# Two softmax attentions of a decoder: where TensorE waits for the copied values, and which queue loads one batch's packed keys

## The reference

```python
q = jnp.einsum('bsd,hkd->bhsk', x, wq.reshape(H, dk, D))
k = jnp.einsum('bsd,hkd->bhsk', x, wk.reshape(H, dk, D))
v = jnp.einsum('bsd,hkd->bhsk', x, wv.reshape(H, dk, D))
q = _apply_rope(q, sin, cos)
k = _apply_rope(k, sin, cos)
scores = jnp.einsum('bhqk,bhsk->bhqs', q, k) / jnp.sqrt(jnp.asarray(dk, x.dtype))
scores = jnp.where(causal, -jnp.inf, scores)
...
x = x + _L1_attn_ref(_layernorm(x, axis=-1), L1_attn_wq, L1_attn_wk, L1_attn_wv, L1_attn_wo)
```

```python
logits = jnp.einsum('bqhd,bkhd->bhqk', q, k) * scale
w = jax.nn.softmax(logits, axis=-1)
attn = jnp.einsum('bhqk,bkhd->bqhd', w, v)
```

## Time and profile before

| | |
|---|---|
| time of one execution, median of 3 runs | 1608.46 us (1607.88 to 1609.58) |
| time of the profiled execution | 1609.24 us |
| its span, first to last instruction | 1607.4 us |
| PE busy | 1131.6 us (70%) |
| DVE busy | 1060.7 us (66%) |
| ACT busy | 496.2 us (31%) |
| POOL busy | 575.2 us (36%) |
| mean granted TensorE clock | 0.870 of full speed |

### The profile page before, as it was taken

One profiled execution on the slowest core, in us unless ns is written; L12 is line 12 of the kernel. 1 busy time (PEld: TensorE's weight loads), 2 busy tenths in 40 slices (PEclk: granted clock), 3 DMA queues, 4 the chain that ended last, 5 costly groups with the idle time before them and its releaser, 6 DMA issues. The chain is left out here.

```text
span 1607.4 us, 21391 instructions
## 1 busy us (share of the span) xinstructions
PE 1131.6 (70%) x6058; PEld 713.9 (44%) x6058; DVE 1060.7 (66%) x1795; ACT 496.2 (31%) x957; POOL 575.2 (36%) x596
## 2 busy tenths in 40 slices
PE   7535547999309695555898896698938788766970
PEld 3212135777105573112465544576724334445860
DVE  6999975873695557998886783410345778745454
ACT  3423322333402252332211302233303346622430
POOL 0046613552655113662000042033431532204746
PEclk9669977999759798998998999799978869986995
DMA  5064347996321403432400162323420140048944
GB/s 190 31 252 144 126 132 223 300 322 240 99 71 30 129 4 131 154 133 105 148 1 0 60 147 30 116 73 115 152 79 1 40 120 4 3 141 232 333 143 121
DMA packets 139682, 195.87 MB, mean 122 GB/s; under 512 B 35632, under 2 KB 99138, under 8 KB 138316
## 3 DMA queue, kind: packets, MB, share of 16 engines
q1 hardware_dynamic: 96636, 144.80, 28.6%
q0 software_dynamic: 12704, 29.36, 6.3%
q10 hardware_dynamic: 30256, 20.65, 4.5%
HBM read 142.80 MB, written 31.72 MB: 109 GB/s over the span
## 5 line engine op out<-in xcount | busy, mean ns | idle before, releaser
L165 POOL TENSOR_SCALAR rstd<-moments 128x4 f32<-128x4 f32 x24 | 6.5, 270 | 402.0 <-DVE moments L148 402.0
L177 PE MATMUL psum<-w_ident,h 128*128 128x128 f32 x144 | 29.5, 386 | 111.3 <-DVE h L155 111.3
L558 PE MATMUL psum<-l1s_read,w_ident 128*128 128x512 f32 x128 | 66.0, 641 | 52.6 <-DVE l1s_read L623 52.6
L558 PE MATMUL psum<-l0s_read,w_ident 128*128 128x512 f32 x128 | 65.1, 634 | 52.6 <-DVE l0s_read L623 52.6
L1906 DVE TENSOR_REDUCE l3x_neg<-psum 128x2 f32<-128x512 f32 x128 | 80.7, 683 | 23.8 <-PE psum L1777 23.8
L1881 ACT ACTIVATE l3x_work<-psum 128x512 f32<-128x512 f32 x128 | 72.5, 598 | 50.9 <-PE psum L1800 50.6
L546 POOL TENSOR_TENSOR l1s_drive<-l1s_du,l1s_bc 128x1024 f32<-128x1024 f32 x32 | 75.3, 2354 | 35.2 <-DVE psum L619 35.2
L546 POOL TENSOR_TENSOR l0s_drive<-l0s_du,l0s_bc 128x1024 f32<-128x1024 f32 x32 | 75.2, 2351 | 35.3 <-DVE psum L619 35.3
L1162 PE MATMUL psum<-l0f_w_in,l0f_xT 128*128 (+1 forms) x224 | 77.3, 468 | 0.1
L177 PEld LDWEIGHTS psum<-w_ident,h 128*128 128x128 f32 x144 | 25.1, 200 | 117.8 <-DVE h L155 115.5
L1037 POOL DMA_INDIRECT l3f_x<-l3f_h_rows,l3f_token_of x64 | 59.3, 927 | 50.3 <-DVE l3f_token_of L1433 28.8
(11 more groups left out here) (641 smaller groups left out, 3160.7 us busy)
## 6 DMA issues: line engine op xcount, KB each, us to landing
l0f_w_in<-in_l0f_w_in SPq DMA_DIRECT2D x56, 352.0 KB
l0s_bc<-l0s_scratch SPq DMA_DIRECT2D x16, 1024.0 KB, 5.2
l1s_bc<-l1s_scratch SPq DMA_DIRECT2D x16, 1024.0 KB, 5.2
l3f_w_in<-in_l3f_w_in SPq DMA_DIRECT2D x32, 384.0 KB
l0f_w_down<-in_l0f_w_down SPq DMA_DIRECT2D x56, 176.0 KB
l2f_w_in<-in_l2f_w_in SPq DMA_DIRECT2D x24, 352.0 KB
l0f_y_rows<-l0f_y ACTq DMA_DIRECT2D x56, 128.0 KB
l3f_w_down<-in_l3f_w_down SPq DMA_DIRECT2D x32, 192.0 KB
```

What stands on the lines that cost most here:

```text
L177: ins = nc.tensor.transpose(m.psum[:, at:at + P], m.h[:, t, k * P:(k + 1) * P], m.ident[:])
L558: ins = nc.tensor.matmul(m.pair(2 + c)[:, cols], lhsT=m.ident[:], rhs=rhs[:, cols], start=start, stop=stop, skip_group_check=True)
```

## The change

It has two parts. First, TensorE no longer waits for ScalarE's value copies before the first natural score: the wait on the projections' banks asks for VectorE's alone, and `v_ready` is waited for ahead of the first transposed score (s = 16). This holds for both attentions. Second, in `l1a_` alone, the keys of batch 1 are loaded from ScalarE's queue: SyncE's second span has only the queries (12 DMAs instead of 24), and ScalarE issues the other 12 after its value copies and before its first exponential.

```diff
@@ -1701,12 +1701,23 @@
                 if span == 0:
 
                     sp.wait_ge(self.ones_ready, 1 if x == self.order[0][0] else 2)
-                last = i == 2 * KD - 1
-                made = ((self.high, i + 1), (self.middle, i + 1), (self.last_split, 1) if last else (self.split, i + 1))
                 for part in range(3):
                     if span == 0:
-                        sp.wait_ge(*made[part])
-                    self.load(sp, span, i, part)
+                        sp.wait_ge(*self.part_made(i, part))
+                    if not (self.causal and span == 1 and x == 1):
+                        self.load(sp, span, i, part)
+
+    def part_made(self, i, part):
+        last = (self.last_split, 1) if i == 2 * KD - 1 else (self.split, i + 1)
+        return ((self.high, i + 1), (self.middle, i + 1), last)[part]
+
+    def load_scalar(self, act):
+        act.wait_ge(self.ones_ready, 2)
+        for part in range(3):
+            for i, (x, _) in enumerate(self.order):
+                if x == 1:
+                    act.wait_ge(*self.part_made(i, part))
+                    self.load(act, 1, i, part)
 
     def gpsimd(self, pool, n, meanwhile):
 
@@ -1853,7 +1864,6 @@
             ins.then_inc(self.turn_filled, 1)
 
         pe.wait_ge(self.ident_ready, 2 if self.causal else 1)
-        pe.wait_ge(self.v_ready, 2)
         make = {"max": natural, "neg": negative, "out": back, "outT": features}
         last = n // self.BLOCK - 1
         for s0 in range(0, n + 40, step):
@@ -1864,6 +1874,8 @@
                     make[kind](i)
             for s in range(s0, s0 + step):
                 if 0 <= s - self.LAG < n:
+                    if s == self.LAG:
+                        pe.wait_ge(self.v_ready, 2)
                     turned(s - self.LAG)
             for s in range(s0, s0 + step):
                 if s % 4 == 2 and 0 <= (s - 22) // 4 < n // self.QUAD:
@@ -1996,8 +2008,7 @@
             src = m.hT if self_attn else m.ctxT[:].unsqueeze(1)
             project_tokens(m, pe, jobs, ("v0", "v1"), lambda k, t: src[:, k, t * P:(t + 1) * P],
                            lambda k, t: w("v")[:, k, :], kc)
-            for k in sorted(jobs.emptied):
-                pe.wait_ge(jobs.emptied[k], jobs.takers.count(k))
+            pe.wait_ge(jobs.emptied["vector"], jobs.takers.count("vector"))
 
             def out(name, batches):
                 pe.wait_ge(a.turn_emptied, a.slot("outT", batches - 1) + 1)
@@ -2029,6 +2040,8 @@
                 nc.scalar.activation(dst, src, ACT.Copy).then_inc(jobs.empty(name), 1)
             act.wait_ge(jobs.emptied["scalar"], 2)
             act.sem_inc(a.v_ready, 2)
+            if a.causal:
+                a.load_scalar(act)
             a.scalar(act)
 
         @block.vector
```

## The result

| | before | changed |
|---|---|---|
| median of the runs | 1606.72 us (7 runs, 1599.07 to 1609.58) | 1595.52 us (7 runs, 1592.99 to 1601.91) |
| time of the profiled execution | 1609.24 us | 1593.85 us |
| its span | 1607.4 us | 1592.0 us |
| PE busy | 1131.6 us | 1123.6 us |
| DVE busy | 1060.7 us | 1060.9 us |

The ratio of the changed kernel to the one before is 0.9941, with a 95% interval of 0.9919 to 0.9963: faster by 9.5 us, between 5.9 and 13.0. The forecast was 1599.9 us with a range of 1597.3 to 1605.5.

What follows compares the result with a forecast made beforehand. SyncE's DMA issuing was taken to bound `l1a_`: 7.7 less 0.6 for the clock gives 7.1 us there, plus 1.4 in `l3x_`, so 1608.46 - 8.5 = 1599.9 us. The range was 1597.3 to 1605.5, at 0.78.

Steps and rivals of the forecast that it cites:

- What bounds `l1a_`: First attention: SyncE's issuing at 0.641 us per DMA, not the transfer, delays batches 1 and 2; moving 12 gains 7.7 us.
- Rivals 1 and 2: `l1a_` loads: the two queues take turns, 1607.0 us (chance 0.10); ScalarE's queue is held up, 1610.5 us (chance 0.05).
- batch 2's start: In `l1a_`: third span's last issue ends at 549.2, lands 3.27 us later, batch 2 starts at 552.5, 7.7 us earlier.
- The clock term in `l1a_`: Slow clock after TensorE's idle times in `l1a_` takes 0.6 us off the gain, between -1.1 and +2.
- Part one in `l3x_`: First scores no longer wait for ScalarE, so the first maximum comes 1.45 us earlier; bounds 0 and 2.3.
- The level: Starting time of the whole-kernel forecast: median of the kernel before, 1608.46 us, less 8.5 us.
- Rival 3: In `l3x_`, the first score's load may land as late as ScalarE: 1601.3 us, within the range, included in the 0.78.
- "Faster" at 0.84: Whole kernel: faster by more than the 3.2 us a measurement can tell, all under 1605.2 us; chance 0.84.

## Why the prediction was right or wrong

**What bounds `l1a_`: right.** The prediction put both waits down to the number of issues on SyncE. All three numbers that followed held, aligned: ScalarE issues from 524.88 (forecast 524.9) at 0.656 us (0.641), batch 1 at 534.54 (534.3), batch 2 at 552.43 (552.5). The kernel with half of the keys confirmed the rate from the other side. The Trainium skill's page "DMA: Bandwidth & Descriptors", section "Issuing engines are not separate DMA queues", says that a second engine saves only the usually small time of starting a DMA. This case agrees with what is saved and not with the size: the 0.64 us of each start set the pace.

**Rivals 1 and 2: excluded.** 12 issues in 7.87 us beside 18 in 11.78 leave room neither for taking turns nor for a queue that is held up. The Trainium skill's page "Perfetto Trace Analysis", section "DMA Instruction — HWDGE (DVE, Sync)", describes a lock on the block that generates descriptors. If it is at work here, these rows put it at 0.02 us for each issue at most.

**Inside batch 2's start: right in sum, wrong in the parts.** The prediction added 24 issues of the old pace and 3.27 us to land. Measured, the third span's 24 issues took 552.45 - (527.00 + 12 x 0.654) = 17.6 us, where before they took 16.34, and the landing 1.82 us instead of 3.27. The errors, +1.3 and -1.45, cancel, so that 552.5 was met is luck. Nearly all of the +1.3 is the second long issue on SyncE, of which the kernel before had one; the prediction's sentence that SyncE's issues kept their pace beside a share of 0.69 overlooked that one. The experiment with four spans was built on the 3.27 and failed on it.

**The clock term in `l1a_`: right in sign, too small on average.** At item 32 the gain is 7.0 us (82.73 before, 75.71 changed, each the mean of four profiles: twice the kernel itself and twice with only GpSimd's addition moved, which `l1a_` doesn't contain). At the stage's end it is 5.7 (138.04 and 132.30), and a single pair of profiles gives 4.0 to 7.5. The forecast was 7.7 for the start and 7.1 for the stage. So the term that I took as 0.6 us, between -1.1 and +2, measures 7.7 - 5.7 = 2.0, its upper bound: 0.7 ahead of item 32 and 1.3 behind it. That all of the 2.0 is the clock is not shown; it is what is left over. In these four profiles of the changed code batch 2 began with no slow stretch, one of 3.4 us, and two of 6.8; the first profile happened to have the first.

**Part one in `l3x_`: the step that failed.** The prediction said 1.45 us, with 0 and 2.3 as bounds. The first maximum came 1.6 us earlier, so the mechanism was right and the term for it nearly so. But the stage gained 3.5 (184.99 against 181.5, the same in every profile), outside the bounds. So the term was sized at 1.45 where it measured 3.5. The bounds held only the time by which the first score can move. What an earlier start does to the clock behind it was priced for `l1a_` and not here, although the trace of before had, 20 us further on, a stall of TensorE with 10.2 us at 0.50 behind it. With the stall taken out of both kernels behind the low part, 0.9 to 1.0 of the further 1.9 us went away; the rest is open.

**The level: the greater part of the miss.** The forecast was made against the three runs shown, 1608.46 us. The same kernel's medians beside later kernels were 1606.21 to 1608.48, with single runs from 1599.07 to 1613.92. Of the 4.4 us between forecast and result, 1.7 are the level of the kernel before (1608.46 - 1606.72), 2.1 are `l3x_`, less 1.4 for `l1a_`, and the remaining 2.0 lie mostly between the two medians' difference, 11.2 us, and the ratio's 9.5. The errors of the two terms thus add up to only 0.7 us: with both stages as measured, 5.7 + 3.5 = 9.2, the forecast from 1608.46 would have been 1599.3, still inside the range. What put the result outside is, for the most part, that the median of three runs was taken as exact: from 1606.72 the range would begin at 1595.6, 0.1 above the measured time. As a ratio the forecast was 0.9947 and the result is 0.9941 and 0.9931; the nearness is in part luck, since the errors in the two attentions have opposite signs. The range's low end of 1597.3 took in the bounds of the terms and nothing for the scatter of the median itself, and it should have had at least 2 us for that.

**Rival 3: excluded.** The load landed in time: the first score stands 2.2 us earlier than before, aligned (1282.66 against 1284.88), and `l3x_` gained more and not less than forecast.

**"Faster" at 0.84: right.** Both intervals of the changed kernel lie wholly below 0.998.

## What to carry to other kernels

Where a chain of many small DMAs comes from one queue with the DMA engines half idle, count issues and not bytes: each issue moved to a free engine's queue brought about its 0.64 us at the next batch's start, and cutting a span's bytes in half brought next to nothing. A term for an earlier start should be followed to the next stall of TensorE, since the stretch at half clock behind that stall can be worth as much as the start itself. And before an idle engine is given work, look at what its neighbour does meanwhile: the same addition cost nothing beside maxima out of PSUM and 3.1 us beside a subtraction in SBUF.

## What the hardware showed that was not expected

- SBUF to SBUF copies issue side by side from two queues at 0.66 us each, against 0.641 on one. 64 KB and 128 KB make little difference: 24 of the one took 552.73 - (527.81 + 12 x 0.654) = 17.1 us, of the other 17.6. Single issues of 1.1 to 2.0 us turn up among those of 0.60, all of them behind batch 1's copies, in every `l1a_` read for it.
- VectorE's low part (f32 in, bf16 out, all in SBUF) took 4.33 us instead of 1.23 beside GpSimd's f32 addition, which took 5.49 instead of 4.53. VectorE's 12 maxima from PSUM took 7.26 us with and without it. The low part ended 1.08 us behind the addition in both kernels.
- After idle times of TensorE of nearly the same length the clock was granted differently: after 2.78 us it stayed at 1.00, after 2.44 it was 0.50 for 3.4 us; after 1.79 in `l3x_` it was 0.50 for 10.2 us, after 2.00 for 3.4. Behind the stall of `l3x_` the length was the same in every profile with the same start of the scores, while in `l1a_` such stretches come and go between profiles of the same code.
